# A two-stream decoder kernel: steps cut at each wait, and step orders written out batch by batch

## The reference

```python
x = _layernorm(x + _L0_attn_ref(x, ...))        # gated convolution mixer
x = _layernorm(x + _L0_xattn_ref(x, ctx, ...))  # cross attention, 16 heads of 64, 77 keys
x = _layernorm(x + _L0_ffn_ref(x, ...))         # 8 experts, top 2, and a shared one
x = _layernorm(x + _L1_attn_ref(x, ...))        # self attention, 16 heads of 16, rope
x = _layernorm(x + _L1_xattn_ref(x, ctx, ...))  # cross attention
x = _layernorm(x + _L1_ffn_ref(x, ...))         # self attention whose keys are split in two sets by a test on q
```

## Time and profile before

| | us |
|---|---|
| median of 3 runs | 1525.58 |
| lowest, highest | 1517.62, 1526.28 |
| span of the profiled execution | 1534.1 |

### The profile page before, as it was taken

One profiled execution on the slowest core, in us unless ns is written; L12 is line 12 of the kernel. 1 busy time (PEld: TensorE's weight loads), 2 busy tenths in 40 slices (PEclk: granted clock), 3 DMA queues, 4 the chain that ended last, 5 costly groups with the idle time before them and its releaser, 6 DMA issues.

```text
span 1534.1 us, 27793 instructions
## 1 busy us (share of the span) xinstructions
PE 1336.9 (87%) x11854; PEld 1103.0 (72%) x11854; DVE 976.1 (64%) x1785; ACT 649.8 (42%) x806; POOL 424.2 (28%) x405
## 2 busy tenths in 40 slices
PE   6899998999999999997799789879978958878885
PEld 6788888888878889995387558747756846646563
DVE  3776758768675447776566836766674546567573
ACT  6554546554533336652344145234423531432413
POOL 5140120301324725665033413703421230000000
PEclk9999999999999999997799799979989965988879
DMA  9361210101052207862002000200200020010000
GB/s 294 138 222 32 48 34 18 47 18 49 4 224 69 93 18 259 275 208 81 1 1 75 28 1 17 79 8 1 75 1 1 12 113 22 22 56 15 1 15 15
DMA packets 46138, 103.33 MB, mean 67 GB/s; under 512 B 4336, under 2 KB 26480, under 8 KB 45120
## 3 DMA queue, kind: packets, MB, share of 16 engines
q1 hardware_dynamic: 42944, 93.18, 18.4%
q0 software_dynamic: 3072, 8.39, 1.7%
HBM read 64.79 MB, written 36.77 MB: 66 GB/s over the span
## 4 chain that ended last, share of the span: by engine, by line
PE 70%; DVE 19%; ACT 5%; issue 2%; POOL 2%; DMA 1%; SPq 0%; another core or an unknown queue 0%; POOLq 0%; DVEq 0%; ACTq 0%
PE ps L816 9%; DVE sm L1832 9%; PE ps L117 7%; PE ps L115 7%; PE ps L116 7%; PE ps L1275 4%; PE ps L1269 4%; PE ps L130 4%; PE ps L1014 4%; PE ps L135 4%; PE ps L131 4%; PE ps L998 3%; ACT m L1695 2%; PE ps L1250 2%; DVE m L1821 2%
## 5 line engine op out<-in xcount | busy, mean ns | idle before, releaser
L1447 ACT ACTIVATE m<-ps 128x1024 f32<-128x1024 f32 (+4 forms) x208 | 166.1, 813 | 288.5 <-PE ps L117 109.5
L1832 DVE TENSOR_REDUCE sm<-ps 128x8 f32<-128x2048 f32 (+1 forms) x128 | 193.5, 1532 | 67.3 <-PE ps L1250 36.6
L1821 DVE TENSOR_TENSOR r<-ps,r 128x512 fp32r<-128x512 f32 (+1 forms) x159 | 116.2, 737 | 135.5 <-ACT r L1447 131.8
L2476 POOL TENSOR_SCALAR sm<-sm 128x2 f32<-128x2 f32 x40 | 8.8, 219 | 697.2 <-DVE sm L1850 697.2
L1447 ACT ACTIVATE r<-ps 128x512 fp32r<-128x512 f32 (+1 forms) x159 | 100.8, 639 | 221.3 <-PE ps L816 120.7
L1695 ACT ACTIVATE m<-ps 128x2048 f32<-128x2048 f32 x64 | 119.6, 1877 | 175.2 <-PE ps L1269 175.2
L816 PE MATMUL ps<-cst,m 128*77 128x128 f32 (+2 forms) x1024 | 137.7, 279 | 17.9 <-DVE m L1821 4.7
L816 PEld LDWEIGHTS ps<-cst,m 128*77 128x77 f32 (+2 forms) x1024 | 115.5, 147 | 42.2 <-issue 15.1
L1250 PE MATMUL ps<-m 32*128 32x256 f32 x1024 | 109.9, 567 | 33.0 <-DVE sm L1832 25.7
L1250 PEld LDWEIGHTS ps<-m 32*128 32x128 f32 x1024 | 67.6, 271 | 67.3 <-DVE sm L1832 49.0
L1269 PE MATMUL ps<-m 32*128 32x256 f32 x1024 | 88.2, 472 | 31.4 <-DVE m L2248 24.0
(11 more groups left out here) (322 smaller groups left out, 3613.8 us busy)
## 6 DMA issues: line engine op xcount, KB each, us to landing
raw<-wu_dram SPq DMA_DIRECT2D x20, 768.0 KB
keep_dram<-m SPq DMA_DIRECT2D x8, 768.0 KB, 3.7
m<-keep_dram SPq DMA_DIRECT2D x8, 768.0 KB, 4.2
xs_dram<-gsq SPq DMA_DIRECT2D x2, 2944.0 KB, 18.1
ys_dram<-m SPq DMA_DIRECT2D x23, 256.0 KB, 2.5
room<-wu_dram SPq DMA_DIRECT2D x7, 768.0 KB, 4.8
rt<-xs_dram SPq DMA_DIRECT2D x16, 256.0 KB, 3.1
w1raw<-w_dram SPq DMA_DIRECT2D x1, 3840.0 KB, 11.8
```

Source lines behind the costliest of these rows:

```text
L1447: return act.activation(o, i, ACT.Copy)
L1821: return dve.tensor_tensor(o, a, b_, op)
L1832: return dve.tensor_reduce(o, i, AX.X, op, **kw)
```

## The change

No arithmetic, tile, buffer or wait is added or removed. Two things are edited.

First, about 50 yields are put in the generators of all four engines, most of them directly ahead of a wait that stood in the middle of a step (between the high and low halves of a projection, between a reduction and what reads it), so that a step ends there. In `fa` the steps of `early` and `front` for the first two batches and the four pieces of `early` for later ones also become steps of their own.

Second, the lists are written out for all batches. `in_turn` now walks one list over the whole stage, so each pair can have its own order.

```diff
 def in_turn(first, second, after):
 
-    n, done = len(after), 0
-    for j in range(4 * n):
-        want = n * (j // n) + after[j % n]
+    done = 0
+    for want in after:
         while done < want:
...
@@ -874,6 +930,7 @@
                 for c in (0, 2):
                     for k in range(2):
                         whole(pe, into[c][0], into[c][1][k], cols(xT, A, k), k == 0)
+                yield
                 pe.wait_ge(*st.l0_dve.at(b, "xT"))
...
@@ -1412,6 +1482,8 @@
                 next(nxt, None)
                 yield
                 yield from project_out(st, b, v, wfp, sig, dve_.at(b, "oT"), dve_.at(b, "oT"), bank(st, 2))
+                yield
+                next(nxt, None)
                 yield
                 next(nxt, None)
...
```

More of the change, by code:

```diff
@@ L58 @@
+    "DVE": [
[4 rows of a table added]
 }
@@ L924, in l0 @@
                         for u in KV0[b][s]:
-                            unit0(*u)
+                            for _ in unit0(*u):
+                                yield
                     elif s < (4 if b < 6 else 3):
@@ L936, in l0 @@
                 for h in range(2):
+                    if h:
+                        yield
                     pe.wait_ge(*st.l0_act.at(b, f"y{h}"))
@@ L1885, in l0 @@
                             yield
+                        elif b:
+                            yield
                 if b == 0:
@@ L1958, in l0 @@
                 for j in range(2):
+                    if j:
+                        yield
                     dve.wait_ge(*pe_.at(b, f"y{j}"))
@@ L1990, in xattn @@
                 for u in range(2):
-                    shift(u)
+                    yield from shift(u)
                     yield
                 for u in range(2):
-                    sums(u)
+                    yield from sums(u)
                     yield
                 for u in range(2, 4):
-                    shift(u)
+                    yield from shift(u)
                     yield
                 for u in range(2, 4):
-                    sums(u)
+                    yield from sums(u)
                     yield
@@ L2045, in norm_only @@
                 if b >= 2:
-                    routed_add(st, b)
+                    yield from routed_add(st, b)
                 yield from layernorm(st, b, st.n_dve, st.n_pool, room=n_room(st))
@@ L2302, in a1 @@
                 yield
-                divide(st, b, v, sig, pe_)
+                yield from divide(st, b, v, sig, pe_)
                 yield
```

60 lines of the change are left out of this document (43 added, 17 removed), and 53 rows, old and new, of tables (FIRST, LAST, SECOND).

## The result

| | before | changed |
|---|---|---|
| median of 4 runs each, us | 1524.34 | 1505.76 |
| lowest, highest | 1517.62, 1526.28 | 1505.0, 1508.33 |
| ratio of the two, 95% interval | | 0.9885 (0.9866 to 0.9904) |
| span of the profiled execution | 1534.1 | 1506.3 |

The change makes the kernel 1.15% faster: by the ratio 17.5 us, with 14.6 to 20.4 in the interval. The forecast was 24.4 us less, 1501 with a range of 1486 to 1523. So direction and range held.

What follows compares the result with a forecast made beforehand. In both self attentions PE is held by hand-overs between engines, with DVE the bound in the maxima. FIRST 0, SECOND 13.0 and LAST 11.4 sum to 24.4 us, taking 1525.6 to 1501.2; range 1486 to 1523.

Steps and rivals of the forecast that it cites:

- FIRST, 0 us: Stretch up to 697 us: same instructions, order and waits, so 0 us; length unchanged to within 1 us.
- Start of pair and layernorm waits: SECOND: interleaved projections fill each other's waits, 0.8 us a pair; qkv fills layernorm waits in two pairs, 1.8 in all.
- The end of the attention: SECOND: s3(3) ahead of t3(2) lets o3(3) start 4.1 us earlier; 2.0 us a pair left, bounds 0 and 4.1.
- T2 side by side: SECOND, DVE: second batch's T2 directly behind the first's starts s0(3) 1.7 us earlier; routed rows eat most in stream 0.
- the clock's rival: Denser attention start in SECOND and LAST brings full clock earlier, 20 us more gain, about 1482 us; chance 0.12.
- The signs named ahead: SECOND: pairs about 3 us shorter, T2 wait from 7.4 to under 3 us, ot wait from 10.9 to about 9.
- Maxima and weights in lockstep: LAST: both batches in step, s0 to o3's end 23 to 26 us; gain 0.1 to 5.8 a pair, 1.4 taken.
- The start: LAST: turning batches 1 and 0 interleaved hides ACT's copies and the wait around them, 3 us; bounds 1 to 4.
- The end: LAST: oT(7) side by side with oT(6) is out earlier, so add(7) comes some 1.4 us earlier.
- Given back at the next queue: DVE and ACT do not follow: SECOND's 2.0 and LAST's 1.4 per pair are lost, about 1515 us; chance 0.25.
- Nothing: Whole kernel: all moves lie in slack, time stays at 1525 us; chance 0.06.
- lockstep costs: LAST: both batches want ACT at once and s0(4) waits for T2(4), 3.8 us a pair; about 1541 us, chance 0.07.

Runs made afterwards that it cites:

- e3: New orders in LAST alone, FIRST and SECOND with the old ones: 1520.1 us, ratio 0.9979 to the kernel before.
- e2: New orders in SECOND alone, FIRST and LAST with the old ones: 1510.6 us, ratio 0.9906 to the kernel before.
- e1: Changed kernel with its yields kept, but lists giving every engine its order of before: 1524.9 us, ratio 1.0008 to the kernel before.
- e6: Old orders, but in SECOND's first three pairs DVE computes both T2 side by side, routed rows behind: 1517.8 us, ratio 0.9959 to the kernel before.
- e9: Changed kernel with T2 apart again in SECOND's first three pairs, PE computing the first batch's s0 twice there: 1506.3 us, ratio 0.9874 to before.
- e8: Old orders, but the end of SECOND's four attentions, from first batch's o3 to the cross attention's first projection, new: 1518.6 us, ratio 0.9958 to before.
- e4: Changed kernel, each maxima group in LAST issuing its first eight matmuls twice: 1505.4 us, ratio 0.9875 to the kernel before.
- e7: Changed kernel, SECOND's third pair ordered like its second, LAST's last pair ending in the old order: 1503.8 us, ratio 0.9880 to before.
- e11: The changed kernel timed and traced again, nothing altered: 1506.0 us, ratio 0.9867 to the kernel before.

## Why the prediction was right or wrong

**Sum.** 24.4 us forecast, 17.5 measured (14.6 to 20.4): the direction was right, and the size was 40% too high. The miss is in LAST: its 11.4 us lie outside what e3 measured (1.2 to 5.3), while SECOND's 13.0 lie inside e2's interval (10.4 to 18.4).

**FIRST, 0 us: right.** The stretch ended at 694.3 us instead of 697.4, outside the 1 us that I had promised; but e1, with the order of before, ends it at 693.6. The yardstick was wrong, not the step: one order spreads by more than 3 us there.

**SECOND, 13.0 us forecast, 14.3 measured by e2 (17.6 between the traces of e1 and e2).** The size was right and its make-up was not, so that it came out is in part luck.

- *Start of pair and layernorm waits, 5.0 us:* from the traces of e1 and e2, everything but the stretch from the first s to the cross attention's first projection shrank by 3.4. That stretch begins behind the first pair's start, so it holds three of the four starts, 4.2 us of the 5.0. Nearly right, though no run changed this part alone. The four waits that the prediction started from left out the two largest of the same view, those for the reductions of the maxima (14.1 and 8.5 us); their term was 0, and that held: from the first mx to the first s a pair took 20.2 us in e1 and 20.2 to 20.5 in e2.
- *The end of the attention and T2, 8.0 us:* from the first s to the first projection the four pairs took 150.9 us in e1 and 136.7 in e2, 14.2 less. The step that failed is "T2 side by side", which I priced as a wait of 1.7 us that the routed rows mostly eat, so at nearly nothing. It gave 6.3 us alone (e6). The mechanism was the one of the clock's rival, placed one step too far off: I wrote that "the maxima ahead of them are as sparse as before", and looked for the cause there; it was the 1.73 us in which PE idles between s0 of the two batches, as e9 shows. The rows that I read could hardly show it: in the third pair of before the clock was back 7.9 us after the first s, the second earliest of the 15 attentions with T2 apart, and in the first two pairs of the same trace after 16.7 and 12.1.
- *The end of the attention:* o3 came 4.1 us earlier by my layout and half of it was to be given back. In e8 the last o was 2.9 us earlier in the first and the third pair, where the clock's return differed by less than 1 us, and 2.4 and 1.4 of it went back, to the turned x, which now stands behind y of the second batch. The two effects were named rightly. Kept were 0.6 and 1.5 us in these two pairs; timed, the four pairs kept 6.4 us, 1.6 each (1.0 to 2.2), so that the forecast's 2.0 is neither confirmed nor excluded. For the end and T2 together the forecast had 8.0; alone they gave 6.4 and 6.3, that is 12.7 of the stage's 14.3.
- *The signs named ahead:* the pairs shrank by 3.6, 5.7 and 7.6 us (e1 to the changed kernel, from maxima to maxima), not by 3; the T2 wait fell to 2.7 as forecast; the ot wait did not fall to 9, it stayed at 11.3.

**LAST, 11.4 us forecast, 3.2 measured by e3 (1.2 to 5.3).** By the means over the traces (five with the old orders, five with the new, e4 left out):

| term | forecast | traces |
|---|---|---|
| start of the stage to the first pair's last o | -3 | +1.4 (68.8 to 70.2) |
| three pair steps with what lies between, and the last attention | -7.0 | -6.3 (196.9 to 190.6) |
| last o to the end | -1.4 | +1.6 (16.6 to 18.2) |

- *Maxima and weights in lockstep* held: in the changed kernel the maxima of the third pair took 26.6 us (22.6 before), and s0 to the last o 23.9, 24.5 and 23.7 in the last three pairs, inside the 23 to 26 forecast, where e1 took 27.0, 29.6 and 27.4. Lockstep does not cost; that rival is out. The gap ahead of nm0(5) was 4.2 us, longer than the 3.2 of the bad end, as xs(5) took 3.6 us; e1 has three gaps there, 5.8 us together. DVE of the changed kernel, and then of e1:

```profile
1382.03 15.70 DVE L1919 TENSOR_REDUCE sm<-ps 128x8 f32<-128x2048 f32 x7 [4.18 <-PE ps L1317]
```

```profile
1392.19 2.29 DVE L1919 TENSOR_REDUCE sm<-ps 128x8 f32<-128x2048 f32 x1 [1.98 <-PE ps L1317]
1397.25 13.39 DVE L1919 TENSOR_REDUCE sm<-ps 128x8 f32<-128x2048 f32 x6 [2.76 <-PE ps L1317]
...
1412.85 2.29 DVE L1919 TENSOR_REDUCE sm<-ps 128x8 f32<-128x2048 f32 x1 [1.09 <-PE ps L1317]
```

- *The start failed.* The first mx did come earlier (12.9 us into the stage instead of 14.3 to 18.8), but I booked that as a gain of the stage. The first pair pays the 3 to 4 us of its lockstep maxima like the others, and in its attention the full clock came back only after 9.5 to 12.7 us, so it took 30.6 to 32.3 us (29.4 to 29.6 with the old order, at 10.2 to 11.2) and got nothing back. The clock is not the whole of it. The list does not put this pair's weights in lockstep: T2(0) stands ahead of the last reduction of batch 1, and s0(1) starts 7.6 to 8.4 us behind s0(0) in the five traces (8.5 in e1), where the third pair has both back to back. And s3(1) starts 6.9 us behind the s before it (4.7 in e1). e7 has the same order here and had the full clock throughout this attention; it still took 29.3 us, where the third pair took 23.5 with the full clock throughout (e3, e9). DVE of the changed kernel, first pair: T2(0), nm3(1), T2(1).

```profile
1261.36 1.22 DVE L1908 TENSOR_TENSOR m<-m,ps 128x1024 f32<-128x1024 f32 x1 [0.78 <-PE ps L869]
1262.49 2.28 DVE L1919 TENSOR_REDUCE sm<-ps 128x8 f32<-128x2048 f32 x1
1265.56 1.22 DVE L1908 TENSOR_TENSOR m<-m,ps 128x1024 f32<-128x1024 f32 x1 [0.79 <-PE ps L869]
```

This term needed the whole pair to be laid out, and I had laid out only the others. No run changed the start alone, so how the 1.4 us split is open; the single traces with the new orders spread by 1.8 us, those with the old by 4.5.
- *The end failed in its sign.* I followed oT(7), which moved up in the order but not in time: it runs 6.5 us behind the last o's end instead of 5.8. DVE in e1, from the last o's end at 1507.04: oT(6), oT(7), add(7), ln(7).

```profile
1508.72 0.69 DVE L1908 TENSOR_TENSOR r<-ps,r 128x512 fp32r<-128x512 f32 x1
...
1512.82 0.66 DVE L1908 TENSOR_TENSOR r<-ps,r 128x512 fp32r<-128x512 f32 x1
...
1515.27 0.69 DVE L1908 TENSOR_TENSOR xres<-ps,xres 128x512 f32<-128x512 f32 x1 [0.49 <-PE ps L189]
...
1518.10 0.74 DVE L1913 TENSOR_SCALAR xres<-xres,sm 128x256 f32<-128x256 f32 x2 [1.14 <-POOL sm L2592]
```

The same four in the changed kernel, from the last o's end at 1487.91:

```profile
1492.60 0.67 DVE L1908 TENSOR_TENSOR r<-ps,r 128x512 fp32r<-128x512 f32 x1
1494.42 0.69 DVE L1908 TENSOR_TENSOR r<-ps,r 128x512 fp32r<-128x512 f32 x1 [1.14 <-ACT r L1520]
...
1497.83 0.69 DVE L1908 TENSOR_TENSOR xres<-ps,xres 128x512 f32<-128x512 f32 x1
...
1500.76 0.73 DVE L1913 TENSOR_SCALAR xres<-xres,sm 128x256 f32<-128x256 f32 x2 [0.28 <-POOL sm L2592]
```

oT(6) went from 1.7 to 4.7 us behind the last o: rc and on of batch 7 now stand ahead of it on DVE, and on PE y(6) stands behind the turning of oT(7). Putting the first batch's finish behind the second batch's start made both late. That is not all of the 1.6 us. With the old orders the end took 16.6 us in all five traces, with the full clock until the last projection was out. With the new, four of five took 18.4 or 18.5, and in these the clock fell 5.0 to 6.0 us behind the last o, where y(6) runs (it starts at 5.4 to 5.5), and came back during y(7); in e11 it did not fall there, and the end took 17.1. So some 0.5 us go with the order at full clock and some 1.3 with the half clock. Whether the order brings that fall on, by PE's waits of 0.68 and 1.48 us ahead of y(6), no run shows; e7, with the old order at the end, had no fall and took 17.0.

**The rivals.** *Given back at the next queue* named the place and the mechanism at the end of SECOND's attention rightly (5.9 to 8.3 us), but not the extent: e8 still kept 6.4 us. Its other half, LAST's gain per pair gone, did not come (6.3 of 7.0 us were there). What was missing in LAST, at its start and its end, no rival had. The total, 1505.8, lies between this rival (1515) and the forecast (1501). *The clock* was right in its mechanism in SECOND, at a third of its 20 us (e6), and its sign for LAST did not come: the granted clock there is 0.81 in the mean of five traces with the old orders (0.79 to 0.82) and 0.81 with the new (0.77 to 0.83). *Nothing* and *lockstep costs* are out.

## What to carry to other kernels

Price a wait of PE by where the clock stands, not only by its length: a gap of 1.7 us in the first groups after a sparse stretch went with twice the time until the full clock (12.7 us against 6.3), and closing it gave 2.1 us a pair (1.4 to 2.8) where the sum had next to nothing. Look at the clock in every pair before choosing the one to read. When two streams are put in lockstep, lay out the first pair and the last one too; the middle ones came out as the timeline said (6.3 us of 7.0), and at the end one stream's finish got stuck behind the other's start. Take a stage's length from several traces of one order before reading a difference of 3 us: two executions of one order differed by up to 6.

## What the hardware showed that I had not expected

- The same order can take two lengths in one place, by when the clock returns: LAST's attentions of the old orders took 29.4 to 29.6 us where it came 10.2 to 11.2 us after the first s, and 27.0 to 27.4 where it came after 1.0 to 2.1 us, in all 20 attentions of five traces, with nothing in between.
- Doubled work can be free, and even repay: the 48 matmuls of e9 stand in a wait, and with them the kernel took 3.8 us less (1506.3 against 1510.1), while the 256 of e4, in the maxima of LAST, brought none (1505.4 against 1505.8).
